# A transformer layer on eight cores: context passes on two pairs of banks, wq issued ahead of GpSimd's sums, LN2 scaling between the Gelus, and ln1_b's part of the context added in the context sums

## What is computed

```
h = layer_norm(x, ln1_g, ln1_b)
q, k, v = h @ wq, h @ wk, h @ wv              # 4 heads of 256
q = softmax(q * scale, axis=-1); k = softmax(k * scale, axis=-2)
context = einsum('bhnd,bhne->bhde', k, v);  attn = einsum('bhnd,bhde->bhne', q, context)
x2 = x + attn @ wo + bo
h = layer_norm(x2, ln2_g, ln2_b)
out = (x2 + gelu(h @ w_ff1 + b_ff1) @ w_ff2 + b_ff2) @ w_d + b_d
x = layernorm(x + out)
x = layernorm(x + (silu(x @ w_gate.T / 127) * (x @ w_up.T / 127)) @ w_down.T / 127)
```

## Time and profile before

| what | us |
|---|---|
| median of three runs | 1409.81 (1409.21 to 1581.51) |
| the profiled execution | 1409.62 |
| its span, slowest core (core 0) | 1408.0 |
| spans of the eight cores | 1402.5 to 1408.0 |
| TensorE busy | 1361.5 |
| VectorE, ScalarE, GpSimd busy | 574.6, 379.5, 190.5 |

### The profile page before, as it was taken

How to read it: one execution, slowest core, us unless ns; L and a number is a source line. 1 busy time by engine, 2 the same in 40 slices (tenths; PEclk the granted TensorE clock), 3 DMA queues, 4 the chain that set the end, 5 groups by cost and what they waited for, 6 DMA issues and landing times.

```text
span 1408.0 us, 17723 instructions; the slowest of 8 cores (1402.5 to 1408.0 us)
## 1 busy us (share of the span) xinstructions
PE 1361.5 (97%) x6484; PEld 629.2 (45%) x6484; DVE 574.6 (41%) x1036; ACT 379.5 (27%) x704; POOL 190.5 (14%) x103
## 2 busy tenths in 40 slices
PE   5969999999997999999999999999999999999997
PEld 4424444445443444444444444444444444444443
DVE  5755666255825121112112555652222222223566
ACT  4622333122760211211221345431111111111225
POOL 0522211306364000000010222200000000000000
PEclk9999999999998999999999999999999999999999
DMA  8464444097765623033010455551030100100113
GB/s 211 130 111 106 98 90 91 8 186 226 137 111 103 130 53 60 0 61 60 1 61 16 85 118 96 162 157 58 0 120 1 61 0 1 60 1 0 60 61 120
DMA packets 104773, 112.95 MB, mean 80 GB/s; under 512 B 90480, under 2 KB 90736, under 8 KB 102000
## 3 DMA queue, kind: packets, MB, share of 16 engines
q1 hardware_dynamic: 101664, 77.68, 21.5%
q0 software_dynamic: 2736, 33.56, 12.4%
q10 hardware_dynamic: 288, 0.59, 0.2%
HBM read 108.66 MB, written 8.39 MB: 83 GB/s over the span
## 4 chain that ended last, share of the span: by engine, by line
PE 91%; DMA 3%; DVE 3%; issue 2%; ACT 2%; DVEq 0%; SPq 0%; ACTq 0%; POOLq 0%
PE P L925 27%; PE P L1111 22%; PE P L896 15%; PE P L413 8%; PE P L471 5%; PE P L1020 4%; PE P L833 4%; PE P L694 2%; PE P L1077 2%; DMA xsA<-xkv 1%; DMA xsB<-xkv 1%; ACT HT L391 1%; DMA S<-wk 1%; PE P L750 0%; PE P L451 0%
## 5 line engine op out<-in xcount | busy, mean ns | idle before, releaser
L925 PE MATMUL P<-S,GB 128*128 128x512 bf16 x1776 | 392.6, 381 | 8.7 <-DVE R L932 8.7
L1111 PE MATMUL P<-T,S 128*128 128x512 bf16 x1408 | 305.7, 379 | 0.0
L932 DVE TENSOR_TENSOR R<-R,P 128x1024 f32<-128x1024 f32 x111 | 135.4, 1220 | 382.7 <-PE P L925 382.7
L925 PEld LDWEIGHTS P<-S,GB 128*128 128x128 bf16 x1776 | 174.5, 98 | 220.7 <-issue 13.1
L896 PE MATMUL P<-T,S 128*128 128x512 bf16 x1024 | 225.1, 379 | 0.2 <-ACT GB L908 0.2
L1111 PEld LDWEIGHTS P<-T,S 128*128 128x128 bf16 x1408 | 137.8, 98 | 166.1
L908 ACT ACTIVATE GB<-P,pv 128x512 bf16<-128x512 f32 x128 | 86.1, 685 | 265.2 <-PE P L896 265.2
L413 PE MATMUL P<-S,HT 128*128 128x512 bf16 x704 | 156.8, 379 | 0.0
L896 PEld LDWEIGHTS P<-T,S 128*128 128x128 bf16 x1024 | 100.1, 98 | 121.3 <-issue 0.7
L1121 ACT ACTIVATE sl<-P 128x512 bf16<-128x512 f32 x88 | 52.4, 596 | 360.8 <-PE P L1111 354.9
L1124 DVE SCALAR_TENSOR_TENSOR GB<-sl,P 128x512 bf16<-128x512 bf16 x88 | 60.5, 688 | 208.3 <-PE P L1111 206.1
(11 more groups left out here) (114 smaller groups left out, 871.0 us busy)
## 6 DMA issues: line engine op xcount, KB each, us to landing
S<-wff POOLq DMA_DIRECT2D x8, 2048.0 KB, 16.1
xsA<-xkv SPq DMA_DIRECT2D x16, 512.0 KB, 5.8
xsB<-xkv SPq DMA_DIRECT2D x16, 512.0 KB, 4.3
R<-xkv SPq DMA_DIRECT2D x16, 512.0 KB, 9.6
xsD<-xkv SPq DMA_DIRECT2D x16, 512.0 KB, 4.3
y<-R SPq DMA_DIRECT2D x14, 512.0 KB, 2.6
S<-wgT SPq DMA_DIRECT2D x2, 2048.0 KB, 13.7
S<-wuT SPq DMA_DIRECT2D x2, 2048.0 KB, 14.5
```

Source lines behind the costliest of these rows:

```text
L925: tk = p.pe(lambda e, hc=hc, hf=hf: e.matmul(P[pr][:, hf * 512:(hf + 1) * 512], gb[:, hc * 512 + tile * 128:hc * 512 + tile * 128 + 128], ...
L932: t_R[i] = p.ve(lambda e: e.tensor_tensor(rrow(i), rrow(i), P[pr][:, :], ALU.add), tk, t_R[i])
L1111: tk = p.pe(lambda e, c=c, hc=hc, b=b, sw=sw: e.matmul(bank(b), S[sw][:, c * 1024 + hc * 128:c * 1024 + hc * 128 + 128], T[:, c * 2048 + t ...
```

## The change

- The scratch for ln1_b in bf16 (`b1b`), its cast and `bwv_mm` go. In `G_last` VectorE first adds ln1_b times `Sbc` to `Ga`, in place, in an instruction of its own (128x512 f32, sixteen in all), then adds the sum from PSUM as before. `ctx` copies its product with one ScalarE instruction.
- The quarter passes of K: tiles 0 to 2 take quarter 2 ahead of tile 3's quarters 0 and 1.
- The loop: K alternates pairs 0 and 1 up to tile 7, and uses pair 0 from tile 8 to 27. Context passes alternate pairs 1 and 2 up to tile 15, and 2 and 3 from then on. The first three `G_add` (ScalarE) come one iteration later, right behind the exponential of K. wq is issued at i = 6, behind the load of x's tile 14, ahead of that iteration's sum on GpSimd.
- `scale_h2` does one column block a call with a token for each. Blocks 2 and 3 are scaled on ScalarE, one call behind each Gelu of `FF1(1)` and `FF1(2)`, instead of on VectorE between tiles of `second(0)`.

```diff
@@ -568,7 +566,6 @@
 
     A1(0)
     A2(0)
-    t_b1 = p.ve(lambda e: e.tensor_copy(b1b[:, :], pv[:, B1:B1 + 8]), t_pv)
     T_tile(0, 1)
     A2(1)
     T_tile(1, 2)
@@ -582,10 +579,10 @@
     K_quarter(2, 1)
     A2(3)
     T_tile(3, 4)
-    K_quarter(3, 0)
-    K_quarter(3, 1)
-    for i in range(4):
+    for i in range(3):
         K_quarter(i, 2)
+    for q in range(3):
+        K_quarter(3, q)
     A2(4)
     T_tile(4, 5)
     for i in range(4):
@@ -607,9 +604,11 @@
             A2(i + 1)
         if i < 11:
             T_tile(i + 1, i + 2 if i < 9 else None)
-        if i == 11:
-            t_wq = load_w("gpsimd", 1, wq_d, 0, t_xt[15])
-        K(i, 0 if own else i % 2)
+        if i == 6:
+            t_wq = load_w("gpsimd", 1, wq_d, 0, t_x[14])
+        K(i, i % 2 if i < 8 else 0)
+        if 9 <= i < 12:
+            G_add(0, i - 9, 1 + (i - 1) % 2)
         if own:
             if last:
                 for f in range(3):
@@ -619,14 +618,14 @@
             Q_exp(i, 1)
             if last:
                 unit(u + 1, 3)
-            G_pass(g - 1, c, 2)
+            G_pass(g - 1, c, 3 - i % 2)
             A(i)
             Q_norm(i)
             Q_tr(i)
-            G_add(g - 1, c, 2)
+            G_add(g - 1, c, 3 - i % 2)
             continue
         if g >= 1:
-            G_pass(g - 1, c, 2)
+            G_pass(g - 1, c, 1 + i % 2)
         if last and g >= 1:
             for f in range(4):
                 unit(u + 1, f)
@@ -637,13 +636,13 @@
                 A1(j + 1)
         if i >= 11:
             A(i)
-        if g >= 1:
-            G_add(g - 1, c, 2)
+        if i >= 11:
+            G_add(g - 1, c, 1 + i % 2)
 
     for i in range(28, 32):
         K(i, 0 if i % 2 == 0 else 1)
-        G_pass(2, i - 24, 2)
-        G_add(2, i - 24, 2)
+        G_pass(2, i - 24, 3 - i % 2)
+        G_add(2, i - 24, 3 - i % 2)
     t_kdone = t_htfree[1]
     t_wv = load_w("gpsimd", 0, wv_d, 0, t_kdone)
     t_wo = load_w("gpsimd", 2, wo_d, 0, t_g[2][7], t_xn[31])
@@ -695,28 +694,21 @@
                 bank(b), xh(j)[:, c * 128:(c + 1) * 128], er(j)[:, hf * 512:(hf + 1) * 512],
                 start=(t == 0), stop=(t == 7)), *w, sig=(t == 7))
         t_g3[0] = tk
+
+        ga = Ga[:, c * 1024 + hf * 512:c * 1024 + hf * 512 + 512]
+        t = p.ve(lambda e: e.scalar_tensor_tensor(
+            ga, Sbc[:, hf * 512:(hf + 1) * 512], pcol(B1, c), ga, ALU.mult, ALU.add),
+            t_Sbc, t_ga[c])
         t_gs[hf][c] = p.ve(lambda e: e.scalar_tensor_tensor(
             gs(c, hf), bank(b), pcol(G1, c),
             Ga[:, c * 1024 + hf * 512:c * 1024 + hf * 512 + 512], ALU.mult, ALU.add),
-            tk, t_ga[c])
+            tk, t)
         free[b] = t_gs[hf][c]
 
     t_CT = [None] * 4
     t_ctx = [None]
 
-    def bwv_mm():
-        b = tbank()
-        for m in range(8):
-            for c in range(8):
-                w = [free[b], t_wv, t_b1] if m == 0 and c == 0 else []
-                tk = p.pe(lambda e, m=m, c=c: e.matmul(
-                    bank(b)[:, m:m + 1], S[0][:, c * 1024 + m * 128:c * 1024 + m * 128 + 128],
-                    b1col(c), start=(c == 0), stop=(c == 7)), *w, sig=(m == 7 and c == 7))
-        t = p.ve(lambda e: e.tensor_copy(iv[:, 8:16], bank(b)[:, 0:8]), tk)
-        free[b] = t
-        return t
-
-    def ctx(h, t_bw):
+    def ctx(h):
         b = next_bank() if h < 2 else tbank()
         hf, o = h // 2, (h % 2) * 256
         for ec in range(2):
@@ -728,12 +720,8 @@
                     gs(c, hf)[:, o:o + 256], start=(c == 0), stop=(c == 7)),
                     *w, sig=(ec == 1 and c == 7))
         t_ctx[0] = tk
-        for ec in range(2):
-            m = 2 * h + ec
-            t = p.ve(lambda e, ec=ec, m=m: e.scalar_tensor_tensor(
-                CT[:, m * 256:(m + 1) * 256], Sbc[:, h * 256:(h + 1) * 256],
-                iv[:, 8 + m:9 + m], bank(b)[:, ec * 256:ec * 256 + 256], ALU.mult, ALU.add),
-                tk, t_Sbc, t_bw, t_qsl[0], t_qsl[1])
+        t = p.se(lambda e: e.activation(CT[:, h * 512:(h + 1) * 512], bank(b)[:, :],
+                                        AF.Identity), tk, t_qsl[0], t_qsl[1])
         t_CT[h] = t
         free[b] = t
 
@@ -785,18 +773,17 @@
 
     for c in range(8):
         G_last(c, 0)
-    t_bw = bwv_mm()
     for c in range(8):
         G_last(c, 1)
         if c == 3:
-            ctx(0, t_bw)
+            ctx(0)
         if c == 5:
-            ctx(1, t_bw)
+            ctx(1)
     for i in range(4, 16):
         load_xc(i, t_g3[0], t_acc[0])
-    ctx(2, t_bw)
+    ctx(2)
     CW(0, (0, 1))
-    ctx(3, t_bw)
+    ctx(3)
     CW(1, (2, 0))
     CW(2, (1, 2))
     CW(3, (0, 1))
@@ -818,7 +805,7 @@
 
     t_xh2 = [None] * 16
     t_xh2free = [None] * 8
-    t_h2 = [[None] * 4 for _ in range(4)]
+    t_h2 = [[None] * 8 for _ in range(4)]
     t_o = [None] * 16
 
     t_opr = [None] * 16
@@ -856,18 +843,17 @@
             "h2%d" % i, dst, xh2[:, (i % 8) * 1024:(i % 8 + 1) * 1024],
             t_xh2[i], t_ctx[0])
 
-    def scale_h2(k, f, eng):
+    def scale_h2(k, c, eng):
 
         ws = [t_h2t[4 * k + j] for j in range(4)]
-        for c in (2 * f, 2 * f + 1):
-            r = T[:, c * 2048 + k * 512:c * 2048 + k * 512 + 512]
-            if eng == "scalar":
-                t = p.se(lambda e, r=r, c=c: e.activation(
-                    r, r, AF.Identity, bias=pcol(B2, c), scale=pcol(G2, c)), *ws)
-            else:
-                t = p.ve(lambda e, r=r, c=c: e.tensor_scalar(
-                    r, r, pcol(G2, c), pcol(B2, c), ALU.mult, ALU.add), *ws)
-        t_h2[k][f] = t
+        r = T[:, c * 2048 + k * 512:c * 2048 + k * 512 + 512]
+        if eng == "scalar":
+            t = p.se(lambda e: e.activation(r, r, AF.Identity, bias=pcol(B2, c),
+                                            scale=pcol(G2, c)), *ws)
+        else:
+            t = p.ve(lambda e: e.tensor_scalar(r, r, pcol(G2, c), pcol(B2, c),
+                                               ALU.mult, ALU.add), *ws)
+        t_h2[k][c] = t
 
 
     t_G = [[None] * 8 for _ in range(28)]
@@ -890,7 +876,7 @@
             b = banks[fk[0] % len(banks)]
             fk[0] += 1
             for c in range(8):
-                w = [t_h2[t][c // 2]]
+                w = [t_h2[t][c]]
                 if c == 0:
                     w += [free[b], t_f1[q]]
                 tk = p.pe(lambda e, c=c, hc=hc, b=b: e.matmul(
@@ -942,7 +928,8 @@
         if i == 12:
             t_bf2 = p.dma("sync", "bi", BI[:, :], bias_d[128:256, :], t_xb[15])
         if i in (6, 8, 10, 12):
-            scale_h2(0, i // 2 - 3, "scalar")
+            scale_h2(0, i - 6, "scalar")
+            scale_h2(0, i - 5, "scalar")
 
     def add_bff2(i):
         t_R[i] = p.gp(lambda e: e.tensor_tensor(rrow(i), rrow(i), BI[:, :], ALU.add),
@@ -955,19 +942,19 @@
     t_f2[1] = load_w("gpsimd", 4, f2_d, 1, t_o[15])
     t_bd = p.dma("sync", "bi", BI[:, :], bias_d[256:384, :], t_R[15])
 
-    for f in range(4):
-        scale_h2(1, f, "scalar" if f < 2 else "vector")
+    for c in range(8):
+        scale_h2(1, c, "scalar" if c < 4 else "vector")
     arot = [6, 7, 4, 5, 0, 1]
     FF1(0, range(8), arot)
     t_f1[2] = load_w("gpsimd", 0, f1_d, 2, t_xh2free[7], t_xh2free[6], t_xh2free[5], t_xh2free[4])
 
     for n in range(12):
-        FF1(n + 1, range(8), frot)
+        for hc in range(8):
+            FF1(n + 1, (hc,), frot)
+            if n < 2:
+                scale_h2(n + 2, hc, "scalar")
         for tile in range(4):
             tk = second(n, tile, s_f2[n // 4], t_f2[n // 4])
-            if n == 0 and tile in (0, 2):
-                for f in range(4):
-                    scale_h2(2 + tile // 2, f, "vector")
         if n == 2:
             t_f2[2] = load_w("gpsimd", 2, f2_d, 2, t_1[3])
         if n == 3:
```

More of the change, by code:

```diff
@@ L188, in build_nc @@
     pv = at("pv", 130, F32, oM)
-    b1b = at("b1b", 8, BF16, oM + 544)
     ln = at("ln", 192, F32, oM + 576)
@@ L203, in build_nc @@
     ident = pv[:, 66:130].bitcast(BF16)
-    b1col = lambda c: b1b[:, c:c + 1]
     pcol = lambda o, c: pv[:, o + c:o + c + 1]
```

## The result

The changed kernel takes 1393.44 us (median of three; 1393.05 to 1393.63), against 1409.51 of the kernel before (1409.21 and 1409.81): a ratio of 0.9886, with an interval of 0.9857 to 0.9914. That is 16 us faster, and less than 2%. The forecast was 1390.0, with a range of 1378 to 1394. The profiled execution of the changed kernel took 1393.63 us. Executions and cores in which a die ran at a lower clock are left out of all comparisons here.

The account below looks back on a forecast made before the run. TensorE was taken as the bound, losing time in few early waits and the slow clock after them: 1408.0 - 3.9 - 12.0 - 1.6 + 9.6 - 11.8 = 1388.3 us of span, plus 1.6 around it, rounded to 1390; range 1378 to 1394.

Parts of the forecast that it names:

- A: Start, quarter passes of K: quarter 2 first removes TensorE's waits for tile 3 and the slow clock; gain 3.9 us.
- B: Context passes: two bank pairs remove copy-out waits, earlier wq removes the long wait; gain 12.0 us, bounds 8.5 and 14.
- The waits named: New K-pass waits: tile 11 for tile 10's exponential, 0.9 us; tile 12 for scalings of transposed columns, 2.2 us.
- C: Context sums: 1.6 us gained by removed products, 9.6 us lost as a new VectorE addition waits for GpSimd's additions of bo.
- The pair: Context sums: the new VectorE addition plus the one behind it, 1.28 us against 1.73 us of TensorE per sum.
- Rival 2: Context sums: new additions held one GpSimd addition at a time, TensorE loses 4.9 us, keeps its clock; 1385.3 us, chance 0.17.
- D: First second-matrix pass: scalings on ScalarE between Gelus remove TensorE's wait and slow clock; gain 11.8 us.
- Rival 4: Feed-forward: Identity between Gelus makes ScalarE reload tables twice each time, 37 us lost; 1427 us, chance 0.02.
- Rival 3: Context passes: ScalarE and VectorE set the pace or wq delays x, gain only 5 us; 1397 us, chance 0.08.
- Rival 1: Context sums: the new VectorE additions are not held by GpSimd; 1380.4 us, chance 0.25.

Follow-up runs that it names:

- the probe: The changed kernel with four extra VectorE instructions, results unread, beside GpSimd's sixteen unbroken additions of b_ff2; 1403.02 us.
- B's own run: The kernel before with only the two bank pairs for context passes, the moved first three copies and the earlier wq; 1400.02 us.
- the version with the late bo: The changed kernel with GpSimd's first four additions of bo held back until the last context sum is done; 1384.54 us, ratio 0.9826.

## Why the forecast was right or wrong

**A** was right in mechanism: three passes of quarter 2 fill the time until tile 3's columns are there, and the clock stays at its upper level, 2.4 GHz. The 48 products took 5.40 us with no gap on the slowest core. Alone it gave 3.0 us by the medians, not 3.9; where the rest went is not shown.

**B** was right in both its halves and in its new waits. From the transposes of tile 10 (59.42 us) to the K pass of tile 14 (97.94) it is now 38.5 us on core 6, where it was 51.5 on core 0: 13.0 gained against 12.0. The waits named, 0.9 and 2.2, were 0.95 and 1.83. A and B together gave 15.0 by the medians, against 15.9.

**C** failed at the step "So I take it as held: its third of the second eight comes up at 317.25 us, runs at 326.4". The step assumed one wait of some 9 us that ends with GpSimd's fourth addition. The runs show instead that each new instruction beside the additions of bo is held until the one addition that is running ends. On core 6 the delays over 0.74 us were 1.83, 1.25, 1.25 and 1.24 in the first run of additions, 1.34 and 1.24 in the second, 8.2 us in all. That the two would contend was right, shown by reading the sums from PSUM. The length of the wait came from a row of another place, and the probe shows that the same instruction is held there to the end: the difference lies in the place and not in the instruction. The net cost came out at 10.3 us on the slowest core against 8.0 forecast, 9.9 by the medians. That it is this near is luck: one wait of 9 us would have been met by the third product alone, where six short ones, a slower pair and a second run of additions added up to about as much.

A second term of C was mis-sized without any collision. The pair was put at 1.28 us, 0.61 of it from the statistics instruction, whose next neighbour does not wait for its result; the new instruction's does, and the pair takes 1.51 us. So the first product waited 0.77 us where the forecast had "no wait".

**Rival 2** (held one addition at a time, chance 0.17) was what happened, and its price of 4.9 us was too small by three terms. It left out the second run of additions, which VectorE runs into only because the first made it late (2.6 us of the 8.2 on core 6, none on core 4). It took the pair at 1.28 us where it takes 1.51: without any collision TensorE waits 2.0 to 2.3 us, which uses up the 1.6 us of the removed products. And it let TensorE keep its clock, which in the stretch from 312 to 324 us was granted at 0.62, with 3.48 us of matmuls in 12 us.

**D** was right: 11.5 to 11.9 us against 11.8, no wait, one table load, scalings of 0.80 us between the Gelus. Rival 4 is out. Rival 3 is out by B's own run, 11.3 us. Rival 1 (not held) is out by the trace after.

## What to carry to other kernels

In this kernel an instruction added to VectorE had to be priced twice: by its own length and by what GpSimd does beside it; if both its tensors are in SBUF, count one delay for each addition of GpSimd that such instructions can meet, at least, and look for further GpSimd work that it meets once it is late. Taking one operand from PSUM, or holding GpSimd's work until later, gave the whole delay back here (0.74 us for each of the sixteen). Price the wait for its result too, where the next instruction needs it: fewer and longer instructions, with the first products behind all sums, brought the stretch from 44.2 to 42.3 us. And a price from a row of the same pair of engines in another stage is not a value: here the same instruction was held 1.2 to 2.0 us in one place and 37 in another.

## What the runs showed of the hardware that was not expected

- The same VectorE instruction (128x512 f32, two tensors in SBUF, 0.74 us alone) took 1.98 to 2.77 us beside GpSimd's additions of bo over the eight cores, and 10.9 and 37.6 us beside those of b_ff2, which have the same shape. A wait of each addition on the one before brought it to 1.27 and 2.65, while the sixteen additions took 40.83 us instead of 36.89; taking away other waits changed nothing. The cause stays open.
- GpSimd pays too: four additions took 10.61 us beside VectorE's, and 9.30 us beside the version that reads PSUM.
- VectorE started an instruction that waits for the result of the one before 0.85 us after it (L699 to L702), and one that doesn't 0.67 us after it (L702 to L699), with instructions of 0.74 and 0.75 us. Eight of them chained took 0.86 us each.
- On core 7 of the version with the late bo a load of w_ff2 took 34.3 us to land, some 16 being the rule, and TensorE waited 12.4 us for it; on core 7 of the version that reads PSUM it waited 2.8 us for the same load. The first is the profiled execution of that version, 1396.75 us; its other three took 1383.45 to 1384.85.

```profile
PE P L908 <- DMA S<-wff: 12.4, 1, 12.4
```
